# A graph network kernel on one core: V tiles ahead of the weights, exponentials by head pairs, and 242 instead of 222 el columns gathered

## What is computed

```python
h = relu(layernorm(x))
el = einsum((h @ W_src + b_src), attn_l); er = einsum((h @ W_dst + b_dst), attn_r)   # 8 heads
v = h @ W_val + b_val
e = leaky_relu(el[src] + er[dst], 0.2)
exp_e = exp(e - segment_max(e, dst)[dst]); denom = segment_sum(exp_e, dst)
x = x + segment_sum(v[src] * (exp_e / denom[dst]), dst)
h = relu(layernorm(x))
# twice: y = segment_sum((h @ W)[src] * norm, dst) + 2 * self loop + b; h = relu(y)
x = x + h
```

## Time and profile before

| | us |
|---|---|
| median of 3 runs | 4117.27 |
| the profiled execution | 4112.79 |
| its span, first to last instruction | 4111.0 |
| PE busy | 3449.2 (84%) |
| POOL busy | 2673.1 (65%) |
| DVE busy | 2248.4 (55%) |
| ACT busy | 1772.4 (43%) |

### The profile page before, as it was taken

The page is one execution under the profiler, slowest core; times in us unless marked ns, Lnnn a source line. Parts: engine busy times, 40 slices in busy tenths (PEclk is TensorE's granted clock), DMA queues, the critical chain, the costliest instruction groups (busy, mean ns, idle before and its releaser), DMA issues.

```text
span 4111.0 us, 53570 instructions
## 1 busy us (share of the span) xinstructions
PE 3449.2 (84%) x14344; PEld 1654.0 (40%) x14344; DVE 2248.4 (55%) x3778; ACT 1772.4 (43%) x4138; POOL 2673.1 (65%) x2801
## 2 busy tenths in 40 slices
PE   5899986777888888897788888888997787888887
PEld 3499943222233333343333333333442333333332
DVE  6599886777778888883222333333552222333346
ACT  4356512444555555454333344444343333344442
POOL 3677611777777777655777777777006777777775
PEclk9999998999999999999999999999998999999999
DMA  8833335777777777665777777777117777777779
GB/s 292 245 67 62 89 98 198 210 210 210 210 210 210 210 211 210 187 205 191 210 210 210 210 210 210 210 211 210 62 67 225 210 210 210 211 210 210 211 209 352
DMA packets 318047, 802.26 MB, mean 195 GB/s; under 512 B 74753, under 2 KB 97811, under 8 KB 316801
## 3 DMA queue, kind: packets, MB, share of 16 engines
q0 software_dynamic: 201856, 631.01, 53.5%
q1 hardware_dynamic: 86421, 114.67, 8.5%
q10 hardware_dynamic: 29580, 54.49, 3.8%
HBM read 712.57 MB, written 88.19 MB: 195 GB/s over the span
## 4 chain that ended last, share of the span: by engine, by line
PE 32%; POOL 23%; issue 20%; DMA 13%; DVE 7%; SPq 1%; DVEq 1%; ACT 1%; POOLq 1%; ACTq 0%
POOL edge L1280 19%; PE mm L1529 8%; DMA rows_wmat<-v_tab,src_group 6%; DMA edge<-h_tab,src_group 5%; POOL rows_wmat L1280 5%; PE mm L1693 4%; PE mm L1621 4%; PE tr L1621 4%; PE sm L1693 4%; PE sm L1566 3%; DVE edge L866 2%; PE tr L1693 2%; PE tr L1524 1%; DVE big L876 1%; PE hist_ps L1693 1%
## 5 line engine op out<-in xcount | busy, mean ns | idle before, releaser
L1280 POOL DMA_INDIRECT edge<-h_tab,src_group x1564 | 1483.5, 949 | 709.8 <-issue 448.1
L1436 ACT ACTIVATE hots<-iota,drel 128x128 f32<-128x128 f32 x1760 | 538.0, 388 | 1174.8 <-PE misc L1693 587.0
L1280 POOL DMA_INDIRECT rows_wmat<-v_tab,src_group x782 | 739.3, 945 | 289.0 <-issue 218.1
L1693 PE MATMUL mm<-edge,hots 128*128 x880 | 445.6, 654 | 183.1 <-SPq L1098 173.6
L1693 PE MATMUL sm<-edge,hots 128*128 x880 | 462.1, 674 | 163.4 <-SPq L1098 159.3
L891 DVE TENSOR_TENSOR big<-big,mm 128x512 f32 x220 | 151.3, 688 | 653.3 <-PE tr L1693 634.5
L891 DVE TENSOR_TENSOR big<-big,sm 128x512 f32 x220 | 151.3, 688 | 636.6 <-PE misc L1693 623.0
L1693 PE MATMUL tr<-edge,hots 128*128 x880 | 395.6, 592 | 0.0
L1693 PEld LDWEIGHTS sm<-edge,hots 128*128 128x128 f32 x880 | 182.8, 215 | 434.7 <-issue 434.7
L1529 PE MATMUL mm<-rows_wmat 128*128 128x512 f32 x784 | 356.1, 598 | 0.0
L1693 PEld LDWEIGHTS mm<-edge,hots 128*128 128x128 f32 x880 | 175.8, 207 | 445.8 <-issue 445.6
(11 more groups left out here) (252 smaller groups left out, 4423.7 us busy)
## 6 DMA issues: line engine op xcount, KB each, us to landing
h_tab<-rows_wmat SPq DMA_DIRECT2D x98, 256.0 KB, 2.0
edge<-h_tab,src_group POOLq DMA_INDIRECT x1564, 3.7
rows_wmat<-low_tab SPq DMA_DIRECT2D x140, 128.0 KB
ht_tab<-rows_wmat SPq DMA_DIRECT2D x49, 256.0 KB
big<-ht_tab ACTq DMA_DIRECT2D x49, 256.0 KB, 2.9
v_tab<-rows_wmat ACTq DMA_DIRECT2D x49, 256.0 KB, 2.9
x_tab<-big SPq DMA_DIRECT2D x49, 256.0 KB, 2.1
rows_wmat<-v_tab,src_group POOLq DMA_INDIRECT x782, 3.7
```

Source lines behind the costliest of these rows:

```text
L1280: pool.indirect_dma_start(ring[:, 2 * u + c, :], None, tab, bass.IndirectOffsetOnAxis(ap=src_group[:, n:n + 1], axis=0)).then_inc(a["rows_ ...
L1436: act.activation(group_hots[:, q % 2, e, :], iota[:, :], ACT.Abs, bias=drel[:, col:col + 1], scale=-1.0).then_inc(a["dist_set"], 1)
L1693: last = pe.matmul(agg_ps[bank][:, :], group_hots[:, q % 2, w % GROUP * 2 + n, :], edge[:, ds(slot[w % OFFS] + n * D, D)], start=(n == 0), ...
```

## The change

1. `GCOLS` is 242, so 540 columns (135 groups) are picked. The gate of the gathers is capped at the last group.
2. The er load is four DMAs ahead of the low loads 104, 108, 112 and 116; the three table stores stand ahead of the low loads 120, 124 and 128.
3. The maximum is subtracted, and the exponential taken, in four pairs of heads instead of two halves of the columns. ACT takes two pairs before V tile 37 and two before tile 38 (one table load, both halves before tile 39 until now). DVE's tail sums wait pair by pair. The store of the weights waits for all four.
4. `V_AT` is 26, 33, 42 (25, 33, 43). All V tiles come ahead of the first piece of the weights; these go through four banks instead of two.
5. DVE's memset of 10555 columns is split: 4299 columns right after the sums, and 782 behind each of its eight place copies. The late 6144 columns are zeroed by ACT, 512 in each of its first twelve steps of the aggregation, and DVE waits for them ahead of step 18's sum.

```diff
-GCOLS = 222
+GCOLS = 242
-V_AT = (V1 + 11, V1 + 19, V1 + 29)
-EXP_AT = (V1 + 25, V1 + 25)
-W_AT = (V1 + 32, V1 + 32, V1 + 33, V1 + 33, V1 + 34, V1 + 34, TILES, TILES)
+V_AT = (V1 + 12, V1 + 19, V1 + 28)
+LATE_AT = 18
+LATE_PIECES = 12
+EXP_AT = (V1 + 23, V1 + 23, V1 + 24, V1 + 24)
-ER_LOAD = 104
+ER_LOAD = (104, 108, 112, 116)
+TABS_OUT = (120, 124, 128)
...
+        w_banks = [tr[0], tr[1], mm[0], mm[1]]
...
-            for half, at in enumerate(halves):
-                did(dve.tensor_tensor(el[:, at, :], el[:, at, :], top[:, at, :], ALU.subtract))
-                marks[f"arg{half}"] = prep[0]
-            dve.wait_ge(std_set, 4)
-            did(dve.reciprocal(dinv[:, :], small[:, 6, :]))
-
-            dve.wait_ge(w_exp, 2)
+            for pair in range(PAIRS):
+                at = slice(2 * pair, 2 * pair + 2)
+                issue(dve.tensor_tensor(el[:, :, at], el[:, :, at], top[:, :, at], ALU.subtract))
+                marks[f"arg{pair}"] = prep[0]
+            settle()
+
             for h in range(H):
+                if h % 2 == 0:
+                    dve.wait_ge(w_exp, h // 2 + 1)
...
+            issue(dve.memset(big[:, J * H:scanned], 0.0))
             dve.wait_ge(w_kept, 32)
...
+            for i in range(0, 4 * CUT.blocks, 2):
+                b, q = divmod(i, 4)
                 n_w = min(P, SP - b * P)
...
+                if i == 0:
                     dve.wait_ge(sums_kept, 16)
-                    did(dve.memset(big[:, 0:scanned], 0.0))
+                issue(dve.memset(big[:, i // 2 * J:(i // 2 + 1) * J], 0.0))
+            settle()
             all_placed(dve)
-            dve.wait_ge(v_sum, TILES)
-            did(dve.memset(big[:, scanned:ringed + W_EXTRA], 0.0))
...
+                        if w == LATE_AT:
+                            dve.wait_ge(late_zeroed, LATE_PIECES)
...
-                        pool.wait_ge(el_masked, (n - EARLY) * 5 // 8 + PACED)
+                        pool.wait_ge(el_masked, min((n - EARLY) * 5 // 8 + PACED, PCOLS // Q))
...
+            for t in range(V1, TILES):
+                for pair in range(PAIRS):
+                    if t == EXP_AT[pair]:
+                        exponentials(pair)
+                value(Step(t, t % HT, TILES, False))
+            for n in range(2 * CUT.blocks):
+                place_odd(n)
...
+                    if n < LATE_PIECES:
+                        act.activation(late[:, n, :].rearrange("p (a z) -> p a z", z=P),
+                                       zeros[:, 0:P].unsqueeze(1).to_broadcast([P, AW // P, P]), ACT.Copy).then_inc(late_zeroed, 1)
...
-            for n, at in enumerate(W_AT):
-                values(at - values_done[0])
+            values(TILES - values_done[0])
+            for n in range(2 * CUT.blocks):
                 turn_weights(n)
```

More of the change, by code:

```diff
@@ L292, in build @@
         ringed = part.at
+        late = big[:, scanned:ringed + W_EXTRA].rearrange("p (n w) -> p n w", n=LATE_PIECES)
+        assert scanned // AW > LATE_AT
         halves = [slice(half * (J // 2), (half + 1) * (J // 2)) for half in range(2)]
@@ L1098, in count_rows, with keep_tab @@
                     sp.sem_inc(a["rows_ready"], told)
+            def keep_tab(n):
+                sp.wait_ge(dve_prep, marks["slots"])
+                tab, cols = ((need_tab, need_i), (slot_tab[0], slotcol_i[0]), (slot_tab[1], slotcol_i[1]))[n]
+                with nc.allow_non_contiguous_dma(reason="one step of the tables per partition"):
+                    sp.dma_start(tab.rearrange("b p -> p b"), cols[:, :]).then_inc(tabs_kept, 16)
             def load_low(s):
@@ L1380, in _, with exponentials @@
             pipelined(act, PCOLS // Q, 4, 0, far)
-            def exponentials(half):
-                at = halves[half]
-                act.wait_ge(dve_prep, marks[f"arg{half}"])
-                act.activation(el[:, at, :], el[:, at, :], ACT.Exp).then_inc(w_exp, 1)
+            def exponentials(pair):
+                at = slice(2 * pair, 2 * pair + 2)
+                act.wait_ge(dve_prep, marks[f"arg{pair}"])
+                act.activation(el[:, :, at], el[:, :, at], ACT.Exp).then_inc(w_exp, 1)
             def place_odd(n):
```

57 lines of the change are left out of this document (24 added, 33 removed).

## The result

The changed kernel takes 4094.89 us (median of 5 runs, 4091.1 to 4099.75), where the kernel before, with two more runs, takes 4117.27 (4113.02 to 4120.65). The ratio is 0.9947, with a 95% interval of 0.9934 to 0.996: faster by 22 us, about half a per cent. The forecast was 4059.9, in a range from 4050 to 4079. **The direction was right, the size was not: 35 us are missing.** The profiled executions are nearer together, 4112.79 and 4099.75 us (spans 4111.0 and 4097.9), so the trace has to account for 13.1 us of gain where 57.4 were forecast.

A forecast was written before the change was run, and what follows sets the result against it. POOL's train of gathers bounds the kernel, so the first V gather's start counts. Gains 11.1 + 4.9 + 10.9 + 30.5 = 57.4 us take the profiled 4112.8 to 4055.4; 4.5 for the median gives 4059.9, range 4050 to 4079.

The forecast's parts named there:

- Step 1: TensorE's picks of el columns: 135 groups instead of 140, 5 x 2.214 = 11.1 us gained.
- Step 2: The er load among the picks' low loads, in four parts: 4.9 us gained, bounds 0 and 4.9.
- Step 3: Three table stores spread over the late picks: no stop of TensorE left, 10.9 us gained, bounds 0 and 10.9.
- Rival A: Table stores cost the same wherever they stand, three short stops as long as one: 4070.8 us, chance 0.17.
- The el gathers at 0 us: 27 gathers behind the picks' last mask, 1.25 us each, hidden by DVE's scans with 2 us to spare.
- rival C: DVE, not POOL, paces the V layer and absorbs the early gain: 4090.4 us, 4111 with further losses; chance 0.05.
- Steps 4 and 5: Between picks and tail passes: 3.0 us from the second carry; with exponentials by head pairs, 11.5 us including that 3.0.
- T: The last mask of the picks of el columns, at 531.0 us before, forecast to move to 504.1.
- Step 6: V tiles ahead of the weights: POOL's V gathers start 32.3 us earlier, 31.3 after 1 us of delay from the weights' store.
- Rival B: V chain held by weights' store, weight gathers, sum store and V stores: 5 to 10 us lost, 4065 to 4070, chance 0.15.
- Step 7: DVE must multiply by when the ring of 12 gathers is full; the train of gathers stands about 0.8 us.
- Rivals C and D: Beside rival C, D: TensorE stays at 1.2 GHz in the V layer, 1.2 us lost a step, slower overall; chance 0.02.

The follow-up runs named there:

- tabs_runs: The change with each table stored as 16-byte runs, one per partition (128 pieces instead of 512), at the same places; 4079.17 us, ratio 0.9912.
- runs_222: tabs_runs with 222 el columns gathered and 560 picked, the split of the kernel before; 4080.65 us.
- before_runs: The kernel before with only its tables laid out in 16-byte runs, stored where they were; 4105.05 us, ratio 0.998.
- spare_a: runs_pace with four extra scratch stores during the picks, words side by side first and words 512 bytes apart last; 4072.74 us, one run.
- tabs_first: The change with its three table stores at groups 1, 2 and 3 of the picks instead of 120, 124 and 128; 4098.4 us.
- tabs_end: The change with its three table stores back behind the last low load; 4089.97 us, ratio 0.9935.
- spare_b: spare_a with the same four extra stores in the opposite order, words side by side last; 4072.62 us, one run.
- runs_pace: The change with tables in 16-byte runs and the el gathers' gate at 1/2 instead of 5/8 group a gather; 4070.86 us, ratio 0.9887.

## Why the prediction was right or wrong

- **Step 1, five groups fewer: right in size** (11.1 forecast, 11.3 between tabs_runs and runs_222); the price set against it was not, see the el gathers.
- **Step 2, the er load in quarters: right.** No gap stands at the quarters; runs_222 has 4.4 us less of picks than before_runs, where 4.9 was forecast.
- **Step 3, the table stores apart: this step failed.** It took the delay behind the three stores (the stop began 5.5 us after the first was issued) for a reserve that one store alone would not exhaust, and forecast 10.9 us gained. The backlog that it divided by three, 14.5 us to 522, isn't in the DMA view of before either: there the engines are idle from 516.5 us on, while TensorE stops until 523.7. In the profile 19.8 us are lost, 8.9 more than before. A single store stops the picks by itself (6.7 us in spare_a), and three together cost only 10 to 11 (tabs_first 9.8, tabs_end 10.3 more than tabs_runs, before_runs 11.0). The bounds of 0 and 10.9 were wrong at the lower end: "a loss would need a store to hold up the low load behind it by more than its 8.9 us of lead", and in spare_b one held it for 11.37. Rival A had three short stops as long as one; they were nearly twice as long (19.8 against 10.9), and its own test, a stop of 3 us or more at each store, was met. What the stores cost is told by before_runs: the 10.9 were there to be had, by another layout instead of another place.
- **The el gathers at 0 us: this step failed too.** They were laid down at 1.25 us each with 2 us to spare; the profile shows 1.43 to 4.98 beside VectorE's passes, and the wait of 13.88 us. The prediction did work out what 0.1 us a gather would cost, and rival C laid the gathers at 1.5 us each, 4.8 us on the path, but it had no row of a gather beside such a pass, and the sum took the price of a gather during the picks. The Trainium skill (GPSIMD Engine Reference, "1. Specifications") says that GpSimd shares its SBUF interfaces with VectorE, and that instructions of VectorE with two SBUF inputs contend; this trace agrees (4.98 and 4.39 us beside passes of 4.66), though beside the scans, which read two operands from SBUF as well, a gather takes only 1.43 to 1.99. By that rule the step should have had a price.
- **Steps 4 and 5, the second carry and the exponentials: right.** The tail passes start at T + 112.0; T + 98.4 was forecast, and the wait above, 13.9 us, is more than the difference. VectorE waits 0.54 us for TensorE at the second carry (3.54 before), and no wait stands ahead of the tail passes (DVE, timeline):

```profile
629.48 6.88 DVE L810 TENSOR_TENSOR edge<-edge 128x1564 f32<-128x1564 f32 x4
636.40 1.60 DVE L817 SCALAR_TENSOR_TENSOR big<-big,edge 128x782 f32<-128x782 f32 x1
```

 The unknown there came out as taken: 6.88 us for 4 x 1564 elements, 1.10 ns each, against the 1.08 chosen and the 2.04 feared.
- **Step 6, V tiles ahead: right in kind, one term mis-sized.** The hold by other traffic was taken at 1 us, bounds 0 and 6.3; it was 11.5, since the weights' store, the weights' gathers and the sums' store together fill the DMA engines (a share of 0.85 to 1.05 from 640 to 670 us). Of the 12.3 us that the copies lose in runs_pace, 3.5 came back when the gathers alone were held, and 6.0 when the sums' store alone stood later; the two need not add up, since a hold came back when the gathers were let go. Rival B named this stretch, but it too priced a single hold, and its mark (a first V gather after 651) would have been met by the first two places alone: 648.0 + 20.3 + 13.6 = 681.9.
- **Step 7, the ring's start: right.** VectorE's first multiplication is at 701.37, 8 us behind the first gather, and the gathers never stand for it (976.2 us from the first V gather to the last, as before). Rivals C and D did not come: the last V gather moved as much as the first, and TensorE's granted clock is 0.94 or more over the V layer (0.94 up to 750 us, 1.00 from there to 1670). Yet C's mark, a last V gather less than 45 us earlier, was met (12.8): like B's, it couldn't tell its own cause from a loss ahead of the first gather.

The two steps that failed and the one that was mis-sized share a fault: each transfer was priced as it stood alone or in the old order, and the change moved all of them next to something else.

So the sum closes: the first V gather was to come 58.2 us earlier, and 58.2 - 20.3 - 13.6 - 10.5 - 1.0 = 12.8, as measured; at the end it is 13.1.

## What to carry to other kernels

A DMA that wrote 512 single words side by side out of different partitions held the loads and stores beside it for 4 to 7 us, in each of the places tried; change its layout, not its place, and if it has to stay, put such stores together. When work moves to another engine's stretch, price it beside the instructions that it will then run with: GpSimd's gathers beside VectorE's passes with two operands in SBUF took up to five times their own time (4.98 us against 0.94). And before shifting a balance between two engines, count what the receiving one can issue at its pace (one gather in 1.25 us here): 242 columns were at that edge and needed the earlier gate of runs_pace, 262 were far past it.

## What the runs showed of the hardware that was not expected

- **Words side by side, words apart.** Rival A leaned on the Trainium skill (DMA: Bandwidth & Descriptors, "Specifications"), by which writes under 512 bytes are read first and written back. That alone doesn't tell these cases apart: the 512 words 512 bytes apart and the 512 pieces of 16 bytes are under 512 bytes as well, and cost nothing that the picks showed. Only the words side by side did. What happens to them on the way stays open.
- **The pace of the gathers differs from profile to profile.** The same 1564 gathers take 948 ns each in tabs_runs' profile and 951 in tabs_first's (the page's groups):

```profile
L1303 POOL DMA_INDIRECT edge<-h_tab,src_group x1564 | 1483.4, 948 | 709.5 <-issue 448.4
```

```profile
L1297 POOL DMA_INDIRECT edge<-h_tab,src_group x1564 | 1487.5, 951 | 709.4 <-issue 448.5
```

 With the 782 of V rows, 3 ns each is 7 us at the end (2346 x 3 ns), as much as many of the edits here are worth. It accounts for tabs_first, whose first V gather comes 9.5 us before the change's and its end only 3.3: its gathers are busy 6.3 us longer. It does so for most of before_runs: first V gather 10.6 us before that of the kernel before, end 1.4 later, gathers busy 8.4 us longer. It may also be why the median and the profiled execution of one kernel stand up to 10 us apart (runs_pace: 4070.86 and 4060.79), but of no kernel are there two profiles, so that isn't shown. What sets the pace stays open. The place of the first V gather in the profile is the steadier measure of what an edit did, the median the measure of what it is worth.
